# A three-layer outer-product network: the first block's products tile by tile, another order in the first steps, and the last layer's small weight part on GpSimd

## The reference, cut to what matters

```python
h = x; outs = []
for i, S in enumerate([128, 128, 128]):
    out = relu(einsum('bfd,bgd,fgs->bsd', x, h, W[i]) + b[i])
    if i != 2:
        h, direct = out[:, :64], out[:, 64:]
    else:
        direct = out
    outs.append(direct)
return concatenate(outs, axis=1).sum(axis=-1)
```

## Time and profile before

| what | value |
|---|---|
| median of 3 runs | 562.94 us |
| the profiled execution's own time | 562.64 us |
| its span | 560.9 us |
| TensorE busy | 550.7 us (98%) |
| VectorE busy | 532.6 us (95%) |
| GpSimd busy | 507.3 us (90%) |
| ScalarE busy | 385.8 us (69%) |
| moved by DMA | 121.76 MB |

### The profile page before, as it was taken

One profiled execution on the slowest core, in us unless ns is written; L12 is line 12 of the kernel. 1 busy time (PEld: TensorE's weight loads), 2 busy tenths in 40 slices (PEclk: granted clock), 3 DMA queues, 4 the chain that ended last, 5 costly groups with the idle time before them and its releaser, 6 DMA issues.

```text
span 560.9 us, 7920 instructions
## 1 busy us (share of the span) xinstructions
PE 550.7 (98%) x2037; PEld 381.6 (68%) x2037; DVE 532.6 (95%) x487; ACT 385.8 (69%) x443; POOL 507.3 (90%) x225
## 2 busy tenths in 40 slices
PE   6999999999999999999999999999999999999997
PEld 3555767777677777767776677777767676776765
DVE  5779999999999999999999999999999999999975
ACT  1475685877758586686777758587686777758563
POOL 1567999999999999999999999999999999999995
PEclk9999999999999999999999999999999999999999
DMA  8999836649195583937649195573927649163001
GB/s 325 412 411 412 348 106 233 255 139 378 47 332 193 168 321 95 343 124 246 247 147 370 41 331 188 187 299 95 360 106 244 264 142 359 52 219 105 1 1 39
DMA packets 29844, 121.76 MB, mean 217 GB/s; under 512 B 3584, under 2 KB 3712, under 8 KB 27776
## 3 DMA queue, kind: packets, MB, share of 16 engines
q1 hardware_dynamic: 29824, 121.52, 59.0%
HBM read 120.98 MB, written 0.52 MB: 217 GB/s over the span
## 4 chain that ended last, share of the span: by engine, by line
PE 82%; DMA 4%; POOL 4%; issue 4%; DVE 3%; SPq 1%; ACT 1%; POOLq 0%; DVEq 0%
PE acc L642 82%; POOL z_lo L309 4%; DMA xwide<-w 3%; DMA xwide<-x 1%; DVE z_whole L454 1%; SPq L318 1%; DVE z_raw L454 1%; DVE z_lo L309 0%; DVE z_psum L454 0%; ACT h L733 0%; POOL squares L578 0%; ACT z_hi L730 0%; DVE sums L486 0%; DVE sums L470 0%; SPq L345 0%
## 5 line engine op out<-in xcount | busy, mean ns | idle before, releaser
L309 POOL TENSOR_TENSOR z_lo<-z_raw,z_hi 128x1024 fp32r<-128x1024 f32 x201 | 476.4, 2408 | 29.2 <-ACT z_hi L730 28.6
L730 ACT CAST z_hi<-z_raw 128x1024 fp32r<-128x1024 f32 x201 | 207.7, 1047 | 90.6 <-DVE z_raw L454 85.3
L454 DVE TENSOR_TENSOR z_raw<-h,xwide 128x1024 f32<-128x1024 f32 x186 | 222.1, 1215 | 3.3 <-ACT h L733 3.3
L642 PE MATMUL acc<-z_hi,w_hi 128*128 128x512 f32 x558 | 201.4, 442 | 0.4 <-POOL w_lo L594 0.4
L642 PE MATMUL acc<-z_lo,w_hi 128*128 128x512 f32 x558 | 176.7, 398 | 1.8 <-POOL z_lo L309 1.5
L642 PE MATMUL acc<-z_hi,w_lo 128*128 128x512 f32 x526 | 167.9, 395 | 0.0
L642 PEld LDWEIGHTS acc<-z_hi,w_hi 128*128 128x128 f32 x558 | 105.0, 188 | 54.2 <-issue 34.0
L642 PEld LDWEIGHTS acc<-z_lo,w_hi 128*128 128x128 f32 x558 | 102.7, 187 | 32.2 <-POOL z_lo L309 8.7
L642 PE MATMUL acc<-z_whole,w_whole 128*128 128x512 f32 x256 | 120.0, 592 | 0.5 <-DVE z_whole L454 0.5
L642 PEld LDWEIGHTS acc<-z_hi,w_lo 128*128 128x128 f32 x526 | 98.7, 188 | 23.9
L309 DVE TENSOR_TENSOR z_lo<-z_psum,z_hi 128x1024 fp32r<-128x1024 f32 x78 | 94.9, 1217 | 1.9 <-ACT z_hi L730 1.1
(11 more groups left out here) (36 smaller groups left out, 163.3 us busy)
## 6 DMA issues: line engine op xcount, KB each, us to landing
xwide<-x SPq DMA_DIRECT2D x160, 512.0 KB, 5.0
xfirst<-x SPq DMA_DIRECT2D x14, 1792.0 KB, 8.9
xfirst<-x SPq DMA_DIRECT2D x16, 256.0 KB, 9.0
xfirst<-x SPq DMA_DIRECT2D x4, 512.0 KB, 11.5
xwide<-w SPq DMA_DIRECT2D x2, 1024.0 KB, 14.0
xfirst<-x SPq DMA_DIRECT2D x2, 768.0 KB, 10.0
w_whole<-w_whole SPq DMA_DIRECT2D x2, 256.0 KB, 12.7
z_raw<-w0c SPq DMA_DIRECT2D x1, 384.0 KB, 6.8
```

The costliest lines, as they stand in the source:

```text
L309: return eng.tensor_tensor(lo[:, 0:n, :], z[:, 0:n, :], hi[:, 0:n, :].bitcast(F32), ALU.subtract)
L454: nc.vector.tensor_tensor(dst, in0, in1, ALU.mult).then_inc(made[kind], 1)
L642: return nc.tensor.matmul(dst, weights, z[0:rows, t - G * g, :], start=first and first_g and t == G * g, stop=final and t == TILES[layer] - 1)
L730: nc.scalar.copy(z_hi[0:rows, slot("PV", pair, par, pos, HI_RING), 0:n, :], src).then_inc(hi_made, 1)
```

## The change: what it does

- Block 0's x comes in 7 transfers instead of 4: slots 0 and 1 together, then each slot alone, a tile a transfer, with the weight parts between them. The bias comes after them.
- VectorE multiplies block 0's layer 0 one tile (512 columns) at a time, with a wait of its own for each (first_product), and the folds are put between: tile 0, fold 0, tile 1, fold 1, tiles 2, 3, fold 2, tiles 4, 5, 6. TensorE waits for each tile's product. The number of columns multiplied is the same.
- WARM is 10 instead of 12.
- ORDER_0 begins with the whole groups 11, 13, 10, 17 (17 was seventh), and 14W stands between 12V and 16P, 18W between 16P and 15P. The wide tiles of block 0 are loaded in that order too. The squares move two positions later on ScalarE and one on GpSimd.
- In step 1 ScalarE does relu1 (h1 of block 0) before it splits layer 2's weights, not after.
- Layer 2's "under" part is made by GpSimd before its low weights, not by VectorE at position 6.

```diff
-ORDER_0 = "11W 13W 10W 12V 16P 14W 17W 15P 18W 19V 00W 01P 02W 03S"
+ORDER_0 = "11W 13W 10W 17W 12V 14W 16P 18W 15P 19V 00W 01P 02W 03S"
-XREP_AT_0, SQUARE_AT_0, SQUARE_LOW_AT_0 = 9, 10, 12
+XREP_AT_0, SQUARE_AT_0, SQUARE_LOW_AT_0 = 9, 12, 13
-UNDER2_AT = (1, 6)
-WARM = 12
+WARM = 10
...
-            load_first(0, xfirst_head_in[0], range(0, 1 + G))
+            load_first(0, xtile_in[0], range(0, 2))
             sp.dma_start(w0_part[0], w0a).then_inc(w0_in[0], 16)
+            load_first(0, xtile_in[1], [2])
             sp.dma_start(w0_part[1], w0b).then_inc(w0_in[1], 16)
-            load_first(0, xfirst_head_in[1], range(1 + G, 1 + 2 * G))
+            load_first(0, xtile_in[2], [3])
+            load_first(0, xtile_in[3], [4])
             sp.dma_start(w0_part[2], w0c).then_inc(w0_in[2], 16)
+            for t in range(2 * G, T0):
+                load_first(0, xtile_in[t], [1 + t])
             sp.dma_start(bias[:], b).then_inc(bias_in, 16)
-            load_first(0, xfirst_in, range(1 + 2 * G, T0))
-            load_first(0, xlast_in, range(T0, 1 + T0))
...
+            def first_product(t):
+                g = t // G
+                rows = rows_of(0, t)
+                dve.wait_ge(xtile_in[t], 16)
+                other = xshift[0:rows, t, :]
+                dst = z_whole[0:rows, slot("W", -1, 0, g, WHOLE_RING), t - G * g, :]
+                nc.vector.tensor_tensor(dst, other if t == T0 - 1 else xfirst[0:rows, 0, :], other, ALU.mult).then_inc(
+                    made["W"] if t == tiles_of(0, g)[-1] else first_half_made, 1)
...
-            products(-1, 0, 0)
+            first_product(0)
             fold(0)
+            first_product(1)
             fold(1)
-            products(-1, 0, 1)
+            first_product(2)
+            first_product(3)
             fold(2)
-            for pos in range(2, len(order(-1))):
-                products(-1, 0, pos)
+            for t in FOLD[2]:
+                first_product(t)
...
                     if isinstance(j, int) and j == 1 and pos == SPLIT2_AT_1:
+                        pool.wait_ge(lo_made["P"], before("P", 1, 0))
+                        pool.wait_ge(square_lo_made, 1)
+                        split_under(2, len(SPLIT0) + 2, w2_lo_made)
                         split_layer(2, len(SPLIT0) + 2).then_inc(w2_lo_made, 1)
...
                     for t in ts:
+                        if isinstance(j, int) and j < 0:
+                            if t == ts[-1]:
+                                pe.wait_ge(made["W"], number + 1)
+                            else:
+                                pe.wait_ge(first_half_made, g + 1)
                         mm = matmul(w, z, t, True, True)
...
+                    if pos == RELU1_AT and has(1, BLOCKS):
+                        relu1(j, par % 2)
                     if isinstance(j, int) and j == 1 and pos == SPLIT2_AT_1:
                         split_layer(2)
-                    if pos == RELU1_AT and has(1, BLOCKS):
-                        relu1(j, par % 2)
```

More of the change, by code:

```diff
@@ L245, in cin @@
         xfirst_in = sem("xfirst_in")
-        xlast_in = sem("xlast_in")
+        xtile_in = [sem(f"xtile_in{t}") for t in range(T0)]
+        first_half_made = sem("first_half_made")
         xfirst_head_in = [sem("xfirst_head_in0"), sem("xfirst_head_in1")]
@@ L404, in products @@
                 if layer == 0:
[L405 to L413, removed]
+                    if isinstance(j, int) and j == 0:
                         if g == 0:
@@ L416, in products @@
                         if g < len(xfirst_head_in):
-                            dve.wait_ge(xfirst_head_in[g], 32)
+                            dve.wait_ge(xfirst_head_in[g], 16)
                         else:
-                            dve.wait_ge(xfirst_in, 32)
+                            dve.wait_ge(xfirst_in, 16)
                     elif g == 0:
                         dve.wait_ge(xrep_ready, j + 1)
[L422 to L426, removed]
+                        dve.wait_ge(xfirst_in, 16 * (j + 1))
+                    in0 = xrep_psum[0:rows, None, :].to_broadcast([rows, n, N])
                     in1 = xshift[0:rows, G * g:G * g + n, :]
-                    if g == len(KINDS[0]) - 1:
-                        in0 = in1
                 elif layer == 1:
@@ L510, in step @@
                     subtract(*p[1:])
[L512 to L519, removed]
             def fold(k):
@@ L600, in split_layer, with split_under @@
                 return split(stage[layer][:, 0:n, :], SPLIT_FROM[layer], n, 128, hi_count)
+            def split_under(layer, hi_count, made_low):
+                under, n = slice(HALF, 128), SPLIT_COUNT[layer] - 1
+                pool.wait_ge(w_hi_made, hi_count)
+                nc.gpsimd.tensor_tensor(w_hi[under, SPLIT_FROM[layer] + n, :], stage[layer][under, n, :],
+                                        w_hi[under, SPLIT_FROM[layer] + n, :].bitcast(F32),
+                                        ALU.subtract).then_inc(made_low, 1)
+                pool.wait_ge(made_low, 1)
             for i, (a, ts) in enumerate(SPLIT0[:-1]):
                 split(w0_of(ts), a, len(ts), 128, i + 1).then_inc(w_lo_made, 1)
-            n = SPLIT_COUNT[1] - 1
-            pool.wait_ge(w_hi_made, len(SPLIT0) + 1)
             pool.wait_ge(w_lo_made, len(SPLIT0) - 1)
-            nc.gpsimd.tensor_tensor(w_hi[HALF:, SPLIT_FROM[1] + n, :], stage[1][HALF:, n, :],
-                                    w_hi[HALF:, SPLIT_FROM[1] + n, :].bitcast(F32), ALU.subtract).then_inc(w1_lo_made, 1)
-            pool.wait_ge(w1_lo_made, 1)
+            split_under(1, len(SPLIT0) + 1, w1_lo_made)
             split_layer(1, len(SPLIT0) + 1).then_inc(w1_lo_made, 1)
@@ L653, in contract @@
                 if kind == "W":
-                    pe.wait_ge(made["W"], number + 1)
+                    if not isinstance(j, int) or j >= 0:
+                        pe.wait_ge(made["W"], number + 1)
                     z = z_whole[:, slot("W", pair, par, pos, WHOLE_RING)]
@@ L747, in copy_xrep @@
                 if isinstance(j, int) and j == 0:
-                    act.wait_ge(xfirst_head_in[0], 32)
+                    act.wait_ge(xfirst_head_in[0], 16)
                 else:
-                    act.wait_ge(xfirst_in, 16 * (j + 2))
+                    act.wait_ge(xfirst_in, 16 * (j + 1))
                 if not isinstance(j, int) or j > 0:
```

2 lines of the change are left out of this document (removed).

## The result

The changed kernel takes 562.11 us in the median of 8 runs (561.73 to 563.03). The kernel before, now with 8 runs, takes 564.65 (562.46 to 564.95). Its runs lie in two groups, 562.5 to 562.9 (3 runs) and 564.6 to 565.0 (5 runs); of the three that were known, 564.83 was in the long one. The ratio is 0.9966 (95% interval 0.9949 to 0.9982), a gain of 0.34%. The forecast of 562.5 within 561.0 to 564.0 holds, and so does "same", within about 0.5% (the far end of the interval is 0.51%). Against the short group, to which the profile before belongs, the change wins 0.5 us (562.64 and 562.15 for the profiled executions); against the median 2.5.

A forecast was written before the change was run, and what follows sets the result against it. The page showed TensorE busy 98%, with GpSimd setting the pace from 54 to 87 us behind a load at 52.06. Terms -0.55 + 0.15 = -0.4 us took 562.64 to 562.2, or 562.5 as median; range 561.0 to 564.0.

The forecast's parts named there:

- The floor: Step 1: the squares' load lands at 52.06 us whatever the engines do, set by bytes, ending the lead except on VectorE.
- the term of 0.55 in the sum: GpSimd's pause before 70 us goes, so TensorE's last wait ends 0.55 us earlier; ends 0 and 0.8.
- the other term: The load at 52 us may come later through smaller transfers: 0.1 to 0.2 us, 0.15 in the sum.
- Those hang on a DMA of the same place in the queue and don't move: Step 0: GpSimd's low weights stay at 23.92 us, TensorE's 0.96 us wait goes, and one of about 0.8 comes at 16P.
- h1 was to begin at 35.7: Into step 1: ScalarE begins h1 at 35.7 us, ready at 37.05; VectorE gains 1.24, or 1.5 with the small part gone.
- GpSimd is ahead by 0.8 us at 45: Step 1: GpSimd starts its first subtraction at 44.4 us, its added 0.5 us of small weight part hidden by idle time.
- 14.1 forecast for the end of step -1: Start: TensorE is done at 14.1 us against 14.86, a lead of 0.75; 1.4 without turns, 0.2 at worst.
- an instruction has a fixed part: Step 1: taking the small weight part off VectorE was estimated to save some 0.3 us.
- (1): Rival: the load at 52.06 us comes earlier or the lead is kept, VectorE's 1.24 to 1.55 come through: 561.2; 18%.
- (2): Rival: three added requests cost 0.6 us each, 1.8 at the load near 52: 563.9, or 564.2 as median; 14%.
- (3): Rival: nothing gained; larger wait at 16P, relu1 held elsewhere, VectorE's lead gone before 65 us: 562.6, median 562.9; 15%.
- (4): Rival: with fewer matmuls at first TensorE falls to its 1.2 GHz clock, +2 to +3 us: 565; 3%.

The follow-up runs named there:

- uncut: The changed kernel with block 0's x loaded in the four pieces of before, products still one tile at a time: median 562.17 us, ratio 0.9963.
- relu_under: The kernel before with relu1 ahead of the split of layer 2's weights and the small weight part on GpSimd: median 561.94 us, ratio 0.9960.
- under_only: The kernel before with only layer 2's small weight part moved from VectorE to GpSimd, ahead of its low weights: median 562.25 us, ratio 0.9965.
- relu_first: The kernel before with only relu1 moved ahead of the split of layer 2's weights in step 1: median 562.22 us, ratio 0.9971.
- no_start: The changed kernel with the loads, products and WARM 12 of before at the start: median 561.96 us, ratio 0.9965.
- under_early: The kernel before with VectorE making layer 2's small weight part one product earlier, at position 5: median 562.63 us, ratio 0.9975.
- best: relu_under with the squares of step 1 at position 12 on ScalarE, not 10: median 560.80 us, ratio 0.9946.
- order_only: The kernel before with only the new order of step 0 and the new places of its squares: median 565.34 us, ratio 1.0019.
- sq_late: The changed kernel with the squares of step 1 at position 12 on ScalarE, not 10: median 561.49 us, ratio 0.9957.
- start_only: The kernel before with only the new start (cut loads, products tile by tile, WARM 10): median 564.48 us, ratio 1.0015.
- again: The kernel before, unchanged, timed and profiled again: 7 runs from 562.42 to 563.12 us, 5 from 564.87 to 565.06, ratio 0.9993.
- under_late: The kernel before with VectorE making layer 2's small weight part one product later, at position 7: median 563.60 us, ratio 0.9988.

## Why the prediction was right, and where it was not

**The floor: right.** In every kernel here in which the squares of step 1 wait for their load and GpSimd then runs without the pause before 70, TensorE's last wait ends one fixed time behind the start of the squares. Where the pause stays, it comes on top:

| kernel | squares begin | last wait ends | difference |
|---|---|---|---|
| after | 52.36 | 86.66 | 34.30 |
| uncut | 52.34 | 86.64 | 34.30 |
| relu_under | 52.19 | 86.47 | 34.28 |
| under_only | 52.17 | 86.46 | 34.29 |
| relu_first | 52.06 | 86.40 | 34.34 |
| no_start | 51.92 | 86.22 | 34.30 |
| before, with a pause of 0.58 | 52.07 | 86.89 | 34.82 |
| under_early, with a pause of 0.45 | 52.32 | 87.04 | 34.72 |

The pauses are the 0.52 and 0.42 by which these two lie above 34.30; the first is the term of 0.55 in the sum. The load's landing itself spreads by 0.4 us over these kernels, whatever their first loads look like; this is the other term (0.15 taken, 0.29 measured). Why it spreads is open; one execution of each doesn't tell a kernel's part from chance. best shows that the load is what holds: with the cast ahead of the squares the last wait ends 32.76 behind them, and 1.28 us sooner than in relu_under.

**What of it was luck.** The two terms give 0.4 us at TensorE's last wait; 0.23 was measured, since the floor term was too small. That the profiled time still came at 562.15 (562.2 forecast) is owed to 0.27 us in the stretch behind, where nothing was edited. And the median of 562.5 was the short profile's forecast plus 0.3. The kernel before has a median of 564.65, so the change gains 2.5 us there and not 0.4. The prediction was near in time because it started from a short run, and the change takes the long ones away for a reason that it didn't have.

**Steps that were off, and did not matter.** The first set off most of the others.

- "Those hang on a DMA of the same place in the queue and don't move" failed: layer 1's weights came 0.9 us later, so the wait near 24 stayed (1.45 us at 24.95), though TensorE had its four groups, and 16P's wait was 1.44 and not 0.8. order_only, in which the loads don't move, shows that the rest of this step was right: the wait near 24 is gone, and 16P's is 0.78.
- h1 was to begin at 35.7 and began at 36.60: the sum took the copy of x as done at 29.85, and with its load it moved by 0.93 us. In no_start, where the load doesn't move, h1 begins at 35.85. So VectorE's lead was 0.33 us at 37.96 and 0.76 from 44.76 on, not 1.24 and 1.5. GpSimd's pause before 70 needed only a few tenths, as under_only shows, so the sum held.
- The new order of step 0 costs part of that lead even where the loads stay: its squares stand ahead of h1 on ScalarE. relu_first, with the squares at their old place, has h1 at 34.91.
- "GpSimd is ahead by 0.8 us at 45" failed: it began its first subtraction at 45.35 (before 45.19), and not at 44.4, right behind the low weights. Its small part took 0.45 us, but the cover that was to hide it had gone, since the split before it came 0.84 us later than forecast (38.54). GpSimd still had 1.57 us to stand for the load at 52, so nothing was lost.
- What came early at the start (14.1 forecast for the end of step -1; the last tile's weights were loaded from 13.33) was given back by 25 us.
- The 0.43 us of a matmul does not come from 3.70 us for eight, which is 0.46 with the modelled end of the last. The term stands all the same: weight loads of whole groups follow one another 0.43 apart (48.79 and 49.22 in the kernel before).

**The step that failed in size.** The small weight part was priced at 0.3 us on VectorE, "an instruction has a fixed part". Its true price was 0.3 us or 2.5, by a tie that the kernel before lost in some 57 of 89 runs (the long group). The profile that was read is one in which the tie was won. The row that tells it was in the trace: 45.20 for VectorE beside 45.19 for GpSimd, and GpSimd's subtraction at 2.54 us where others take 2.38. The prediction had found the same turn-taking at 10.78 and had named the rule in the Trainium skill (SBUF — State Buffer, Who interferes with whom), but did not ask where else VectorE reads both inputs from SBUF while GpSimd works. Nor did it weigh that 564.83 stood among the three runs shown.

**The rivals.** (1), the floor passed, did not happen in the change; sq_late and best show that it takes another edit. (2), cut requests delaying the load at 52, needed a delay of 0.55 us there; 0.29 was measured, and uncut has it too, though the cut does delay the loads at 17 and 30. (3) did not occur: the wait at 16P was larger, as it says, but GpSimd's pause went. (4), the clock, did not occur in the change (0.999 or 1.000 in all 8 runs), but it did in 6 of 12 runs of start_only, which has the new start without the new order of step 0.

## What to carry to other kernels

- Find every VectorE instruction with both inputs in SBUF near a long GpSimd instruction, and compare their start times. If they are close, the kernel's time can be a lottery, and the order of the recorded starts doesn't tell who wins; the durations do. Move the short one to where GpSimd idles, or to GpSimd. A short instruction can cost the length of the long one.
- Two or three runs don't show two groups. An outlier of 2 us among three runs is worth a second profile, in the group that the first didn't show.
- When work is moved at the start of a kernel whose loads fill the queue, ask which later load an engine waits for with others queued behind it. Here the squares of step 1, two places later in ScalarE's list, were worth 1.1 us (relu_under 561.94, best 560.80), and the new start nothing.

## What the runs showed of the hardware

Two instructions, a VectorE one with both inputs in SBUF and a GpSimd subtraction, that start within 0.01 us of each other can go either way from run to run, and the price is one-sided: 0.29 us of VectorE's work became 2.50 behind GpSimd's subtraction (again), while GpSimd lost only 0.18 (2.54 against 2.36) when VectorE was first (before). VectorE, coming 1.14 us into the subtraction, took 1.39 (under_late). No wait is shown for it: the time held is inside the instruction's own duration. And for VectorE's products with one input in PSUM, as its other products beside GpSimd from step 0 on have, nothing of the kind is seen: 1.22 us each, beside a GpSimd at work and beside an idle one.

Cutting block 0's x from four requests into seven made a load behind them in the full queue land 0.91 us later (18.06 against 17.15); with the four requests again it came at 17.32.
